# Second layer of a two-layer graph network: one register load per 20 steps of TensorE, of 30 words, in place of two of 20

## What is computed

```python
def _L1_gnn_ref(feat, eweight, W, b, src, dst):
    msg = feat[src] * eweight
    agg = jax.ops.segment_sum(msg, dst, num_segments=n)
    deg = jax.ops.segment_sum(jnp.ones((src.shape[0],)), dst, num_segments=n)
    h_neigh = agg / jnp.maximum(deg, 1.0)[:, None]
    h = jnp.concatenate([h_neigh, feat], axis=-1)
    return h @ W.T + b
...
h = jnp.maximum(_layernorm(x, axis=-1), 0.0)
x = x + _L1_gnn_ref(h, edge_weight1, L1_gnn_W, L1_gnn_b, src, dst)
```

## Time and profile before

| | us |
|---|---|
| median of 3 runs (1586.26 to 1593.48) | 1588.04 |
| the profiled execution | 1572.35 |
| its span | 1570.5 |
| PE busy (78% of the span) | 1230.7 |
| DVE busy (68%) | 1072.8 |
| ACT busy (57%) | 894.9 |
| POOL busy (52%) | 822.8 |

### The profile page before, as it was taken

One profiled execution on the slowest core, in us unless ns is written; L12 is line 12 of the kernel. 1 busy time (PEld: TensorE's weight loads), 2 busy tenths in 40 slices (PEclk: granted clock), 3 DMA queues, 4 the chain that ended last, 5 costly groups with the idle time before them and its releaser, 6 DMA issues. The chain is left out here.

```text
span 1570.5 us, 22072 instructions
## 1 busy us (share of the span) xinstructions
PE 1230.7 (78%) x5128; PEld 906.0 (58%) x5128; DVE 1072.8 (68%) x2592; ACT 894.9 (57%) x2608; POOL 822.8 (52%) x859
## 2 busy tenths in 40 slices
PE   5885488788888888888888876488878878878876
PEld 3453366566666665666664464276656666666654
DVE  5464378777778778878877895366666666665656
ACT  1121287667777777778676373255555555555540
POOL 2004366556666666666650205466666666666660
PEclk8998699989999999999999887699999999999988
DMA  6125456656666666666663013233333333333322
GB/s 169 42 77 161 122 154 177 169 159 174 173 185 169 167 173 182 182 178 186 173 166 118 21 41 114 61 92 89 98 90 97 86 99 95 87 93 93 99 85 89
DMA packets 78855, 195.60 MB, mean 125 GB/s; under 512 B 15687, under 2 KB 34668, under 8 KB 78734
## 3 DMA queue, kind: packets, MB, share of 16 engines
q0 software_dynamic: 53952, 169.45, 39.3%
q1 hardware_dynamic: 21272, 21.56, 4.6%
q10 hardware_dynamic: 3510, 3.20, 0.6%
HBM read 180.91 MB, written 13.24 MB: 124 GB/s over the span
## 5 line engine op out<-in xcount | busy, mean ns | idle before, releaser
L691 POOL DMA_INDIRECT ring<-qv_tab,v_src x440 | 434.4, 987 | 377.9 <-PE bank L814 159.9
L1401 POOL DMA_INDIRECT y_ring<-y_tab,e_idx x380 | 367.1, 966 | 292.0 <-PE bank L1500 117.1
L752 ACT ACTIVATE ring<-ring 128x65 f32<-128x65 f32 x1720 | 431.7, 336 | 0.0
L1550 DVE SCALAR_TENSOR_TENSOR kx<-bank,rdeg,kx 128x256 f32 x440 | 212.7, 483 | 234.4 <-PE bank L1500 174.5
L1481 PE MATMUL bank<-y_parts,src_hot 128*128 128x512 f32 x900 | 282.6, 446 | 93.2 <-ACT src_hot L1436 35.6
L800 PE MATMUL bank<-kx,hotT 128*128 x880 | 257.8, 421 | 121.4 <-issue 60.2
L1435 ACT ACTIVATE src_hot<-src_off,piece_id 128x640 fp32r<-128x640 f32 x180 | 149.2, 829 | 249.4 <-PE bank L1481 91.4
L800 PEld LDWEIGHTS bank<-kx,hotT 128*128 128x128 f32 x880 | 174.8, 207 | 184.7 <-issue 158.5
L814 PE MATMUL bank<-ring,hot 128*128 128x265 f32 x880 | 274.9, 413 | 7.9 <-DVE acc L989 3.8
L1500 PE MATMUL bank<-y_ring,hot 128*128 x880 | 248.7, 406 | 37.9 <-SPq L1424 12.8
L1481 PEld LDWEIGHTS bank<-y_parts,src_hot 128*128 128x128 f32 x900 | 175.2, 199 | 146.7 <-ACT src_hot L1436 57.2
(11 more groups left out here) (257 smaller groups left out, 932.6 us busy)
## 6 DMA issues: line engine op xcount, KB each, us to landing
ring<-qv_tab,v_src POOLq DMA_INDIRECT x440
qv_tab<-qv_out SPq DMA_DIRECT2D x25, 264.0 KB, 2.1
y_ring<-y_tab,e_idx POOLq DMA_INDIRECT x380
y_tab<-acc SPq DMA_DIRECT2D x12, 256.0 KB, 2.6
out_dram<-kx ACTq DMA_DIRECT2D x24, 128.0 KB
xs<-in_x_dram SPq DMA_DIRECT2D x4, 640.0 KB, 14.5
kx<-in_x_dram SPq DMA_DIRECT2D x4, 640.0 KB
src_i<-in_src_dram SPq DMA_DIRECT2D x36, 64.0 KB
```

Source lines behind the costliest of these rows:

```text
L691: pool.indirect_dma_start(one_step(r, 0, PITCH), None, qv_tab, bass.IndirectOffsetOnAxis(ap=v_src[:, r:r + 1], axis=0)).then_inc(got[r % R ...
L752: A.activation(part, part, ACT.Copy, scale=one_step(r, EX + h, EX + h + 1)).then_inc(scaled, 1)
L1401: pool.indirect_dma_start(y_ring[:, e % RH, :], None, y_tab, bass.IndirectOffsetOnAxis(ap=e_idx[:, e:e + 1], axis=0)).then_inc(y_got[e % R ...
L1550: V.scalar_tensor_tensor(row, bank[r % SB][:, 0:D], rdeg[:, bass.ds(tiles[r % U], 1)], row, ALU.mult, ALU.add).then_inc(sums_added, 1)
```

## The change

The two tables become one, `e_step`, of 22 rows of 30 words: a row holds the ring places of 20 steps and, behind them, the 10 counts of the odd ones among them, which are the only counts that were read. One TENSOR_LOAD of 30 words stands where the two of 20 words stood. PE's waits use the same numbers as before, from other registers. `TILES` is set to `U` = 20, so that the loads of node tiles in the first layer stay what they were; the diff touches their code alone in its spelling. Nothing else changes on any engine.

```diff
+    WORDS = LOADED + LOADED // 2
+    TILES = U
...
-        e_place = sb("e_place", [1, STEPS], I32)
-        e_count = sb("e_count", [1, STEPS], I32)
+        e_step = sb("e_step", [1, STEPS // LOADED, WORDS], I32)
...
-                    V.tensor_scalar(e_count[:, :], r_row[0:1, :], 1.0, None, ALU.add)
+                    V.tensor_scalar(e_step[:, :, LOADED:WORDS], r_row[0:1, 1::2].rearrange("o (c n) -> o c n", n=LOADED // 2), 1.0, None, ALU.add)
...
-                    V.scalar_tensor_tensor(e_place[:, :], rounds[:, :], float(-RH), r_row[0:1, :], ALU.mult, ALU.add)
+                    V.scalar_tensor_tensor(e_step[:, :, 0:LOADED], rounds[:, :].rearrange("o (c n) -> o c n", n=LOADED), float(-RH),
+                                           r_row[0:1, :].rearrange("o (c n) -> o c n", n=LOADED), ALU.mult, ALU.add)
...
                     if r % LOADED == 0:
-                        _, places = nc.values_load_multi_w_load_instructions(e_place[0:1, bass.ds(r, LOADED)], engines=[pe.engine],
-                                                                             min_val=0, max_val=RH - 1, skip_runtime_bounds_check_because='the remainder of the edge tile by RH')
-                        _, counts = nc.values_load_multi_w_load_instructions(e_count[0:1, bass.ds(r, LOADED)], engines=[pe.engine],
-                                                                             min_val=1, max_val=ET, skip_runtime_bounds_check_because='one more than the edge tile of a step')
+                        _, words = nc.values_load_multi_w_load_instructions(e_step[0:1, r // LOADED, :], engines=[pe.engine],
+                                                                            min_val=0, max_val=ET, skip_runtime_bounds_check_because='places are remainders by RH, counts one more than an edge tile')
...
                     if r % 2 == 0:
-                        pe.wait_ge(landed, counts[r % LOADED + 1] & 1023)
-                    T_.matmul(bank[r % SB][:, 0:D], hot[:, r % HR, :], y_ring[:, bass.ds(places[r % LOADED], 1), :], start=True, stop=True).then_inc(sums_done, 1)
+                        pe.wait_ge(landed, words[LOADED + r % LOADED // 2] & 1023)
+                    place = nc.s_assert_within(words[r % LOADED], 0, RH - 1, skip_runtime_bounds_check_because='the remainder of the edge tile by RH')
+                    T_.matmul(bank[r % SB][:, 0:D], hot[:, r % HR, :], y_ring[:, bass.ds(place, 1), :], start=True, stop=True).then_inc(sums_done, 1)
```

More of the change, by code:

```diff
@@ L66, in gnn_kernel @@
     LOADED = 20
+    WORDS = LOADED + LOADED // 2
+    TILES = U
+    assert STEPS % LOADED == 0 and LOADED % 2 == 0 and STEPS % TILES == 0
     qv_tab = nc.dram_tensor("qv_tab", (NT * P, PITCH), F32, kind="Internal").ap()
@@ L601, in _, with load_node_tiles @@
                 pairs(body, [read_edges, staircase, select, nothing, read_dst, read_src, read_wgt, read_starts, read_reach, read_rows, read_turned_src, split_biases])
-        def load_node_tiles(eng, i):
-            _, vals = nc.values_load_multi_w_load_instructions(t_int[0:1, bass.ds(i * U, U)], engines=[eng.engine],
+        def load_node_tiles(eng, i, n=U):
+            _, vals = nc.values_load_multi_w_load_instructions(t_int[0:1, bass.ds(i * n, n)], engines=[eng.engine],
                                                                min_val=0, max_val=NT - 1, skip_runtime_bounds_check_because='T(t) is clamped by its construction')
@@ L800, in spread_k @@
                         mm = T_.matmul(spread_bank[n % 3][:, (u % 2) * D:(u % 2 + 1) * D], hotT[:, g % 2, u, :],
-                                       kx[:, bass.ds(tiles[(g * Q + u) % U], 1), :], start=True, stop=True)
+                                       kx[:, bass.ds(tiles[(g * Q + u) % TILES], 1), :], start=True, stop=True)
                     mm.then_inc(k_spread, 1)
@@ L855, in _ @@
                 pe.wait_ge(tables_set, 1)
-                tiles = load_node_tiles(pe, 0)
+                tiles = load_node_tiles(pe, 0, TILES)
                 turn_hot(0)
@@ L876, in _ @@
                     if g + 1 < GR:
-                        if (g + 1) % PER == 0:
-                            tiles = load_node_tiles(pe, (g + 1) // PER)
+                        if (g + 1) * Q % TILES == 0:
+                            tiles = load_node_tiles(pe, (g + 1) * Q // TILES, TILES)
                         spread_k(g + 1, 0, tiles)
@@ L1374, in gnn_kernel @@
         OWN_EVERY = STEPS // NT
-        assert RH % 2 == 0 and LEAD <= HR - 4 and STEPS % LOADED == 0 and RH > NT - 1 + 8
+        assert RH % 2 == 0 and LEAD <= HR - 4 and RH > NT - 1 + 8
         y_ring = tb("y_ring", [P, RH, D])
```

## The result

The changed kernel is slower: 1629.6 us in the median of 4 runs (1619.54 to 1656.44) beside 1590.76 us (1586.26 to 1599.49) of the kernel before. The ratio is 1.0248, with a 95% interval of 1.0177 to 1.0319. Executions of one kernel on this sort of chip differ by up to 3%, the longer ones at a lower granted clock.

The account below looks back on a forecast made before the run. PE was taken to bound the last stage, busy 83%. Savings capped by idle time summed to 11.6 us, less 0.7 for a gather: 10.9, taken as 11 off 1588.04, giving 1577.0 us, range 1568 to 1589.

Parts of the forecast that it names:

- the bound of the new load: PE's one 30-word load in the last stage takes between 1.36 us (fixed time) and 2.04 us (growing with words).
- the middle value of 1.70 us: Time taken for PE's 30-word load, as having both a start and a part for each word; saves 1.02 us.
- the first term: At PE's register loads in the last stage: one load replaces two of 1.36 us, saving 1.02 us each time.
- The right mechanism: Rival, chance 0.05: PE's 30-word loads pay ACT's 0.22 us a word, 6.6 us each; 1638 to 1669 us.
- the case against it: Against that rival: ACT's words are 16-bit on another engine; 32-bit loads on PE and DVE have medians near 0.068 us a word.
- The point of turning: PE's new load turns the change from gain to loss at 2.72 us, 0.091 us a word.
- The idle windows: PE's idle time in 3.20 us windows from 21 load pairs, 15.92 us in all, caps what shorter loads can gain.
- Its matrices move forward with PE: In the last stage ACT, busy 294 of 553 us, mostly waits for PE, so its matrices come earlier when PE does.
- It is given back: Rival, chance 0.31: PE waits longer for ACT's matrix and DVE's sum; 1584 us if two thirds is swallowed, 1588 if all.
- First pair: PE's loads at 953.1 us, at the start of the last stage, are hidden by the gather: nothing gained.
- table writes: DVE's writes in the first stage, once: at most 0.6 us more, at best 0.3 us less; nothing taken.
- order of work: Counts waiting on landed stay the same; SP, POOL, ACT and DVE queues keep their rows; no wait is added.

Follow-up runs that it names:

- row_of_32: Changed kernel with table rows 32 words apart, still 30 loaded, each row at a multiple of 128 bytes: 1562.9 us, ratio 0.9969 to the kernel before.
- load_of_24_again: Changed kernel with 24-word rows, PE waiting for landed once in 5 steps, not 2, on the slower chip: 1586.96 us, ratio 0.9994 to the kernel before.
- table_shifted: Changed kernel with the whole table e_step moved 8 bytes further on; one execution, 1613.7 us.
- load_of_24: Changed kernel with 24-word rows, PE waiting for landed once in 5 steps, not 2, on a faster chip: 1311.36 us, ratio 0.9944 to the kernel before.

## Why the prediction was wrong

**The step that failed** is the bound of the new load: "the time grows with the words, 30/20 x 1.36 = 2.04 us" as the upper end, and with it the middle value of 1.70 us on which the sum stood. It left the address out. All loads of 20 words in the trace begin 80 bytes apart, so all begin alike, and that they agree within 0.01 us said nothing about rows of 120 bytes. Even an aligned load is outside the bounds: 2.36 us, because of the two words beyond the seventh unit. And the fixed start, for which the middle was taken, is only 0.08 us. So the first term, a saving of 1.02 us in each group, is in truth 0.36 us in half of the groups and a loss of 4.36 us in the other half.

**The right mechanism was among the rivals, at 0.05.** It was read off ACT's load, 24 words of 16 bits in 5.27 us, 0.22 us a word, and said that a row "which no longer begins at a multiple of 80 bytes" might be read in that way. The unaligned loads take 0.236 us a word, their start included. It was priced for all rows, 1638 to 1669 us; with half of them it is 1629.6, below that range. The chance was too low. The one row of the trace whose size was not 20 words of 32 bits was also the one that was far off, and the change was about to leave that size and that spacing: a row that is dear and unexplained is worth more than 1 in 20. In the case against it, the argument from the medians of the 20-word loads was no evidence, since none of them tests another address. The Trainium skill, page "Runtime: NRT & Kernel Launch", section "Instruction fetch mechanics", puts about 200 ns on each register; the page speaks of register loads from HBM, and the tables here lie in SBUF. It was set aside because the trace had 0.068. For the unaligned loads it is near: the runs show 0.233.

**The point of turning was right.** The load costs more than 2.72 us on average (106.6 / 22 = 4.85), and the sign is the other one.

**The idle windows** as a measure: in the direction of longer loads they find most of it. The windows of the long loads hold 41.5 us of idle time and those of the short ones 4.5, and PE stands still for 8.7 us at the last load (timeline): 54.7 us beside the 15.9 of before, 38.8 more. The stage as a whole has 31.3 us more of idle time, because 7.5 us come back at other waits, and 14.4 us more of busy PE, which the windows don't count.

In the direction of shorter loads it stays open how good they are. For row_of_32 (0.36 us less in each group) they give 12 x 0.36 + 0.22 = 4.5 us; the ratio of 0.9969 is 4.9 us, with an interval from 13 us less to 3 us more. For load_of_24_again they give about 11 and the idle time at the loads did fall by 12.3, but the time fell by 0.0006 of itself, with an interval of -0.5% to +0.4% that leaves out the 11 us (0.7%). 6.9 us came back before the picking matmuls and about 3 us were lost at the start, which the coarser wait of that run adds. "Its matrices move forward with PE" was said of ACT; the part until ACT grew by 2.2 us only, so this sentence is not what the rows speak against. "It is given back" had 0.31: in that run it was the better account of the time, and no run shows it alone. On the faster chip 12.3 of 22 us came through in the 20 groups, and 7.4 us in the measured time.

**First pair, table writes, order of work:** as forecast. The first load, 2.37 us, is covered by the first gathers (the first matmul comes 4.7 us after it, at 964.23, as with the pair before), and the stages before show no change that can be told from the spread of the runs.

**Why the slowdown is as large as the added load time**: 46.1 us more of loads, 45.7 us more of stage, of which 31.3 are idle time and 14.4 the same matmuls taking longer at the lower granted clock. By the medians of the runs it is 38.8 us (28 to 51 by the interval), so that "one to one" is not shown more closely than this. In the windows of 7.60 us around the long loads PE has only 1.55 to 6.23 us of work in hand. A pair of 2.72 us was bridged by that lead in eight groups of 21; 7.08 us are bridged in none of the ten, and the other engines wait for PE in turn.

## What to carry to other kernels

When register loads are joined or their tables laid out anew, count the 16-byte units and look at where each row begins: rows padded to a multiple of 4 words made the difference between 2.5% slower and no slower, and fewer words, not fewer loads, is what makes them cheap. Before costing an instruction from rows of one size, ask in what they are all alike (length, type, address), and give the odd row that differs in one of these the weight of a real case. Time that the sequencer of the fullest engine lost was mostly paid here, while time that it gained came through only in part: 12 of 22 us on one sort of chip, nothing that could be measured on the other. And where a test needs a second edit to make room for the first (here a coarser wait), look for the price of that edit in the trace before the result is put down to the first.

## What the runs showed of the hardware that was not expected

- A register load (TENSOR_LOAD) from a place that is no multiple of 16 bytes is 3.0 to 3.5 times as long: 30 words 7.08 us in place of 2.36, 20 words 4.75 in place of 1.36. A load of 32 words is shorter than one of 30 (2.13 and 2.36 us).
- In all runs but table_shifted the last load of the stage is longer by 0.4 to 2.7 us than its like (1.97 beside 1.36 before, 9.75 beside 7.08, 3.34 beside 2.36, 3.78 beside 1.62). It falls into the time in which the output is stored; the cause was not tried.
- The same kernel takes 1567.51 and 1590.25 us, at two times, on one chip and 1317 on two others. The loads are alike on both sorts (1.617 us in load_of_24). What differs in the last stage is mostly PE's idle time: load_of_24 has 44.8 us of it there in a stage of 496.8 us, load_of_24_again 134.2 in 617.2, and PE is busy 452.0 and 483.0 us. On the faster chip the page of load_of_24 has

```profile
span 1309.6 us, 21918 instructions
...
L1485 PE MATMUL bank<-y_parts,src_hot 128*128 128x512 f32 x900 | 271.5, 432 | 14.8 <-DVE y_ring L1531 14.0
...
L1503 PE MATMUL bank<-y_ring,hot 128*128 x880 | 235.5, 392 | 27.4 <-SPq L1428 23.8
```

where on the other the same two groups have 106.4 and 24.4 us of idle time (page, whole span), 131 in all in place of 42; and the granted clock is 0.966 there, 0.917 here. What causes it is open; it means that a ratio holds for the sort of chip it was taken on.
